# Layer 1's message sweep of a four-layer graph network: the one-hots of the look-up compared by `tensor_tensor` with the partition number as a broadcast 32-bit operand, instead of by `tensor_scalar` with it as a scalar

## The reference

```python
xl = x @ W_lin + b_lin
s_i = xl @ W_att[:hc]
s_j = xl @ W_att[hc:]
alpha = s_i[row] + s_j[col] + b_att
alpha = jnp.where(alpha >= 0, alpha, 0.2 * alpha)
amax = jax.ops.segment_max(alpha, row, num_segments=n)
alpha = jnp.exp(alpha - amax[row])
asum = jax.ops.segment_sum(alpha, row, num_segments=n)
alpha = alpha / (asum[row] + 1e-16)
msg = alpha[:, :, None] * xh[row]
out = jax.ops.segment_sum(msg, col, num_segments=n)
```

## Time and profile before

| | us |
|---|---|
| median of 3 runs | 5295.33 |
| span of the profiled execution | 5289.8 |
| message sweep of layer 1, from the first gather to the last scaling of rows | 2273.4 to 2827.3 |
| VectorE busy in the whole span | 2794.9 |
| GpSimd busy in the whole span | 3461.7 |

### The profile page before, as it was taken

One profiled execution on the slowest core, in us unless ns is written; L12 is line 12 of the kernel. 1 busy time (PEld: TensorE's weight loads), 2 busy tenths in 40 slices (PEclk: granted clock), 3 DMA queues, 4 the chain that ended last, 5 costly groups with the idle time before them and its releaser, 6 DMA issues.

```text
span 5289.8 us, 73813 instructions
## 1 busy us (share of the span) xinstructions
PE 2873.2 (54%) x17389; PEld 2236.2 (42%) x17390; DVE 2794.9 (53%) x6391; ACT 791.8 (15%) x3180; POOL 3461.7 (65%) x3922
## 2 busy tenths in 40 slices
PE   5443477763333573034445877768986665643333
PEld 5333366653333463034443333356464333543333
DVE  8889822223221588033335988876147666971111
ACT  2121100000000100000001555456100001640000
POOL 3777677767777777777774777654047773017775
PEclk9999955555555555556556999878997766876566
DMA  2211222231112483033333444534169997732223
GB/s 62 67 29 47 68 52 52 52 46 26 27 27 25 60 115 47 18 69 79 81 81 59 137 127 127 133 91 139 40 191 316 335 331 221 268 124 52 52 52 53
DMA packets 303759, 526.16 MB, mean 99 GB/s; under 512 B 89450, under 2 KB 172640, under 8 KB 296928
## 3 DMA queue, kind: packets, MB, share of 16 engines
q1 hardware_dynamic: 177960, 289.53, 19.3%
q0 software_dynamic: 125728, 235.82, 18.3%
HBM read 423.29 MB, written 101.80 MB: 99 GB/s over the span
## 4 chain that ended last, share of the span: by engine, by line
POOL 42%; issue 28%; DVE 14%; PE 9%; DMA 2%; ACT 2%; DVEq 2%; POOLq 1%; SPq 1%; ACTq 0%; PEldq 0%
POOL work L789 31%; POOL rec_by_dst L749 6%; PE ps L2330 3%; POOL acc L789 2%; DVE acc L1568 2%; ACT work L1934 1%; DVE work L1027 1%; PE ps L2104 1%; POOL idx_slot L783 1%; PE ps L2045 1%; DVE work L1015 1%; PE ps L2401 1%; DVE work L973 1%; DVE work L1042 1%; DVE acc L1496 1%
## 5 line engine op out<-in xcount | busy, mean ns | idle before, releaser
L789 POOL DMA_INDIRECT work<-t_h,idx_slot x832 | 801.2, 963 | 546.2 <-DMA t_h<-acc 304.5
L2045 PE MATMUL ps<-work 128*128 128x128 f32 (+1 forms) x2496 | 700.0, 443 | 677.2 <-DMA work<-t_v,idx_slot 352.0
L789 POOL DMA_INDIRECT work<-t_v,idx_slot x832 | 789.2, 949 | 267.0 <-issue 221.9
L2045 PEld LDWEIGHTS ps<-work 128*128 128x128 f32 x2496 | 583.2, 328 | 700.5 <-issue 700.5
L789 POOL DMA_INDIRECT work<-t_xl,idx_slot x416 | 413.5, 994 | 123.8 <-issue 111.0
L2298 PE MATMUL ps<-big,work 128*128 x832 | 411.3, 647 | 105.7 <-DVE work L1246 68.9
L749 POOL DMA_INDIRECT rec_by_dst<-sc_rec_d,sc_idx x392 | 394.1, 1005 | 113.2 <-issue 104.6
L749 POOL DMA_INDIRECT rec_by_src<-sc_rec_s,sc_idx x392 | 388.6, 991 | 113.3 <-issue 104.2
L2370 PE MATMUL ps<-big,work 128*128 x832 | 326.4, 549 | 191.7 <-DVE aS L1630 153.5
L1102 DVE COPY relw<-rec_s 128x16 f32 x104 | 19.7, 189 | 672.8 <-PE ps L2045 672.2
L789 POOL DMA_INDIRECT work<-t_kv,idx_slot x208 | 201.3, 968 | 257.7 <-DMA t_kv<-big 173.1
(11 more groups left out here) (480 smaller groups left out, 6177.0 us busy)
## 6 DMA issues: line engine op xcount, KB each, us to landing
work<-rows_of_v_by_position SPq DMA_DIRECT2D x52, 1024.0 KB
work<-relT_by_dst SPq DMA_DIRECT2D x156, 256.0 KB
rows_of_h_by_position<-work SPq DMA_DIRECT2D x52, 512.0 KB
work<-rows_of_h_by_position SPq DMA_DIRECT2D x52, 512.0 KB
rows_of_v_by_position<-work SPq DMA_DIRECT2D x26, 1024.0 KB
rows_of_v_by_position<-acc SPq DMA_DIRECT2D x26, 1024.0 KB
work<-t_v,idx_slot POOLq DMA_INDIRECT x832
work<-relT_by_src SPq DMA_DIRECT2D x52, 256.0 KB
```

Source lines behind the costliest of these rows:

```text
L789: nc.gpsimd.indirect_dma_start(to, None, table, bass.IndirectOffsetOnAxis(ap=idx_slot[:, h * HU + k:h * HU + k + 1], axis=0)).then_inc(s_g ...
L2045: ins = M.matmul(psum_blocks[:, ds(b, 1), 0:width], oh[:, s, :], ring[:, h * HU + k, 0:width].unsqueeze(1), start=False, stop=False)
```

## The change

One statement is replaced in the first part of a half on VectorE. The wait for the load of `relB` stays where it was, the semaphore increments stay the same, and the output buffer and its type (bf16) stay too. Only the instruction is another one: a `tensor_tensor` of `relB` (bf16) and `pidx` (float32), whose one column is read 1024 times with a step of zero. It is issued 52 times, once a half. The other callers of `rel_one_hots` (layers 1 and 2) keep the scalar form. No instruction changes its place on any engine.

```diff
             def messages_first(i, h):
                 s = h % 2
                 dve.wait_ge(ph("L1C_looked"), half_no(i, h) + 1)
-                rel_one_hots("L1C", i, h, ohTb[:, s, :]).then_inc(ph("rel_used"), 1)
+                dve.wait_ge(s_relB[s], rel_count("L1C", i, h))
+                V.tensor_tensor(ohTb[:, s, :], relB[:, s, :], pidx[:, 0:1].to_broadcast([P, HU * P]), ALU.is_equal).then_inc(ph("rel_used"), 1)
                 dve.wait_ge(ph("L1C_product"), half_no(i, h) + 1)
                 one_hots(oh[:, s * HU:(s + 1) * HU, :], 1, i, h).then_inc(ph("L1C_onehot"), 1)
```

## The result

The changed kernel takes 5334.46 us (median of 5 runs, 5333.02 to 5338.98) beside 5297.46 us for the kernel before (5 runs, 5293.97 to 5299.59). The ratio is 1.0074, with a 95% interval of 1.0061 to 1.0086: 37 us more by the medians and 39 by the ratio (32 to 46), where 38 were forecast. Its profiled execution has a span of 5332.7 us.

What follows compares the result with a forecast made beforehand. The prediction took GpSimd's back-to-back issue of gathers to bound the sweep. Direct holds of 22.5 us and slips of 15.5 us made 38 us, so 5295 + 38 = 5333 us, range 5312 to 5349.

Steps and rivals of the forecast that it cites:

- What bounds the sweep: In the changed sweep GpSimd issues gathers back to back: 409.9 us of gathers and 119.2 us idle, of 550 us.
- The price of the instruction: On VectorE the new comparison takes 1.22 us, 0.74 us more a half, which fits into line 1092's wait for TensorE.
- The rival at 0.69 us: The new VectorE instruction runs at 0.69 us and mostly ends before the index copy: 5298 to 5310 us, chance 0.08.
- The hold on GpSimd: Gathers starting inside a VectorE instruction with two SBUF operands end 0.81 us after it; index copies end 0.04 after.
- Direct holds: GpSimd's index copies wait for the new instruction: 1.73 us in four halves, 22.5 us over 13 passes.
- Slips: Delayed copies move later gathers into lines 1092, 1445 or the new instruction, bringing 22.5 us to 38.
- the walk: Stepping gathers through four halves against VectorE: 0.10 + 1.81 + 1.2 + 0.10 = 3.2 us a cycle, taken as 3.1.
- The rival of no hold: The new tensor_tensor keeps GpSimd from nothing, so the copies' present holds vanish: 5294 us, no change, chance 0.08.

Runs made afterwards that it cites:

- the busy filler on VectorE: The kernel before, with VectorE also copying 640 numbers out of PSUM into scratch behind each scalar comparison: 5296.9 us, ratio 1.0003.
- the two kernels without holds by line 1092: Line 1092's row of numbers put into PSUM, in the kernel before (5282.2 us, ratio 0.9985) and in the changed kernel (5304.6 us, ratio 1.0029).
- two pieces of 0.70 us: The changed kernel with its new comparison cut into two tensor_tensor instructions of 512 elements each: 5325.7 us, ratio 1.0063 to the kernel before.

## Why the prediction was right, and where a step of it was not

- **What bounds the sweep.** Right: GpSimd's back-to-back issue. The result appears in GpSimd's instructions and nowhere else, and the busy filler on VectorE costs nothing (1.0003).
- **The price of the instruction.** Taken as 1.22 us, measured 1.229. The reason given, the operand's 32 bits, is not what decides: a 16-bit column is as slow (1229 ns). The rival at 0.69 us is out.
- **The hold on GpSimd.** Right and isolated: the operand in PSUM removes it all (0.9998). Copies end 0.04 and gathers 0.81 us after the instruction that holds them, as read from the rows of before.
- **Direct holds, 22.5 us.** Measured 22.1 by the copies' sum, and 22.4 as the difference of the two kernels without holds by line 1092.
- **Slips, 15.5 us.** Measured 13.5 by the gathers. But the walk that gave them has a wrong step: "the rows for a half have arrived some 6.9 us after its last gather was issued". In the code the copy of the next half's indices stands between the fourth and the fifth gather, so the gather ahead of a copy isn't the half's last; that is the fourth behind it. Line 1439 starts 1.68 us after that one ends: 2445.90 for 2443.10 + 1.12, and 2462.26 for 2459.64 + 0.94 in the changed kernel. So when the third gather loses a place, the rows arrive a place later too, and with them lines 1446, 1429 and the next 1092. The forecast had the new instruction stay at 10.03 and hold the eighth gather for 0.56; in fact it moves to 11.29 (2465.36), spares that gather and holds the next copy, which takes 1.06 us for 0.20. It had line 1092 catch the second gather of the following half; in fact it catches the third (2469.31, 1.56). The two halves come to 11.50 + 11.54 us, against 12.06 + 11.5 by the forecast. The half behind them was forecast at +0.10, with its third gather ahead of line 1092; it slips in 7 of the 13 passes, as at 2480.26. Averaged over the passes behind the first, the four halves are 1.33, 0.92, 0.54 and 0.03 us longer than before, 2.8 in all, against 1.81, 1.2, 0.10 and 0.10, 3.2 in all. The second of these averages holds what the forecast left out, that the four seventh gathers caught before (1.99 us) are free now. Too much in two halves and too little in the third nearly cancel: that the wrong walk gave the right sum is luck and not reasoning.
- **The times.** 38 us were forecast, and the medians give 37, the ratio 39. The traces give 35.6 to 36.1 for the sweep, so some of the agreement to 1 us is chance as well. (In the chances, 0.55 + 0.17 + 0.12 and a quarter of 0.08 are 0.86 and not 0.87.)
- **The rival of no hold** is refuted: gathers and copies both wait for a `tensor_tensor` with two SBUF operands. The Trainium skill (SBUF — State Buffer, "Who interferes with whom") infers that `tensor_tensor` leaves the generation of descriptors alone; here the trace disagrees, with a gather of 1.86 us for 0.94 beside line 1092. The prediction had that inference free all of GpSimd, which goes further than the Trainium skill does: the same section says that an instruction with two SBUF inputs contends with those of GpSimd that read SBUF, and for the copies, which read their indices there, the trace agrees (1.06 us for 0.20).

## What to carry to other kernels

Where GpSimd issues DMAs back to back, each VectorE instruction with two SBUF operands, and the scalar form of this comparison too, was a lock on it: ask what of GpSimd starts while it runs, not how long VectorE is busy. An operand that stays constant can lie in PSUM at the same speed (1221 ns for 1225), which is worth 7 to 8 us here for line 1092 alone. A delay in such a chain can also move a later start into another lock, and then costs again, 0.8 us a time here (25.0 us in 31 halves); so walk two or three rounds of the rhythm, with every event tied in the code to the instruction that really releases it.

## What the runs showed of the hardware that was not expected

A copy of GpSimd that waits for VectorE gets in between two VectorE instructions back to back: with the scalar form twice (0.88 us from the start of the pair at 2453.80 to its end) no copy took over 0.36 us, and with two pieces of 0.70 us none over 0.67 behind the sweep's start. And a `tensor_tensor` of three bf16 operands takes 1229 ns for 1024 elements when one of them is a single repeated column, against 692 ns in line 969, whose operands are all read in runs of neighbouring numbers.
